# Linear attention with a sign-weight projection: where the next span's LayerNorm affines stand on VectorE

## What is computed

```python
xn = _layernorm(x, axis=-1)
x = x + _L0_attn_ref(xn, Wq, Wk, Wv, Wo, Wb, bb) + _L0_ffn_ref(xn, weights, scale, bias)
...
def _L0_attn_ref(x, Wq, Wk, Wv, Wo, Wb, bb):
    q = (x @ Wq).reshape(B, L, H, Dh)
    k = (x @ Wk).reshape(B, L, H, Dh)
    v = (x @ Wv).reshape(B, L, H, Dh)
    beta = jax.nn.sigmoid(x @ Wb + bb)
    q = _l2norm(q)
    k = _l2norm(k)
    scores = jnp.einsum('blhd,bthd->bhlt', q, k)
    scores = scores * beta.transpose(0, 2, 1)[:, :, None, :]
    mask = jnp.tril(jnp.ones((L, L), dtype=scores.dtype))
    scores = scores * mask
    out = jnp.einsum('bhlt,bthe->blhe', scores, v).reshape(B, L, Dm)
    return out @ Wo
...
def _L0_ffn_ref(x, weights, scale, bias):
    w = (weights >= 0.0).astype(x.dtype) * 2.0 - 1.0
    y = jnp.einsum('bsi,oi->bso', x, w)
    y = y * scale + bias
    y = jnp.clip(y, -MAX_VAL, MAX_VAL)
```

## Time and profile before

| what | us |
|---|---|
| three runs | 1038.15, 1105.11, 1131.73 |
| their median | 1105.11 |
| profiled execution | 1037.92 |
| its span, slowest core (core 4) | 1035.6 |
| its spans, all cores | 1025.6 to 1035.6 |
| PE busy with matmuls | 863.0 (83%) |
| VectorE (DVE) busy | 476.4 (46%) |
| ScalarE (ACT) busy | 280.0 (27%) |

### The profile page before, as it was taken

The page is one execution under the profiler, slowest core; times in us unless marked ns, Lnnn a source line. Parts: engine busy times, 40 slices in busy tenths (PEclk is TensorE's granted clock), DMA queues, the critical chain, the costliest instruction groups (busy, mean ns, idle before and its releaser), DMA issues.

```text
span 1035.6 us, 14710 instructions; the slowest of 8 cores (1025.6 to 1035.6 us)
## 1 busy us (share of the span) xinstructions
PE 863.0 (83%) x5228; PEld 388.9 (38%) x5320; DVE 476.4 (46%) x900; ACT 280.0 (27%) x521; POOL 62.0 (6%) x97
## 2 busy tenths in 40 slices
PE   0008978998999988998999988998989988998995
PEld 0003344433443344433443334433543344434442
DVE  1022375624852365525663365525762365523662
ACT  0003355124122323134132323134223323134110
POOL 9200010000000000000000000000000000000001
PEclk9999977999999999999899989999999989999998
DMA  8962030230134003230134003330134003300135
GB/s 159 168 121 82 0 102 22 59 105 1 41 74 131 1 1 83 62 103 1 41 79 126 1 1 82 61 103 1 41 80 125 1 1 82 82 1 1 41 82 122
DMA packets 21126, 63.90 MB, mean 62 GB/s; under 512 B 3648, under 2 KB 3648, under 8 KB 21056
## 3 DMA queue, kind: packets, MB, share of 16 engines
q0 software_dynamic: 11840, 29.40, 16.9%
q1 hardware_dynamic: 9216, 33.56, 9.1%
HBM read 54.60 MB, written 16.78 MB: 69 GB/s over the span
## 4 chain that ended last, share of the span: by engine, by line
PE 76%; DVE 7%; DMA 4%; ACT 4%; issue 3%; POOL 3%; DVEq 1%; ACTq 1%; POOLq 0%
PE pBig L500 23%; PE pBig L835 12%; PE pBig L625 11%; PE pBig L817 9%; PE T L692 5%; DMA scale_pp<-fsc 4%; PE T L766 4%; PE T L521 4%; DVE sT L784 3%; PE pBig L828 2%; DVE vt L653 2%; PE T L748 2%; PE T L559 1%; ACT xnT L472 1%; PE T L703 1%
## 5 line engine op out<-in xcount | busy, mean ns | idle before, releaser
L784 DVE TENSOR_TENSOR sT<-T,mask 128x512 bf16<-128x512 f32 x256 | 164.4, 684 | 106.0 <-PE T L766 106.0
L835 PE MATMUL pBig<-signT,xnT 128*128 128x512 bf16 x474 | 123.9, 401 | 5.3 <-issue 3.2
L817 PE MATMUL pBig<-Wo,ctxT 128*128 128x512 bf16 x490 | 122.2, 388 | 2.0 <-issue 1.1
L500 PE MATMUL pBig<-xnT,Wq 128*128 128x512 bf16 x503 | 121.6, 385 | 1.7 <-ACT xnT L472 1.4
L500 PE MATMUL pBig<-xnT,Wk 128*128 128x512 bf16 x504 | 119.8, 380 | 0.4
L625 PE MATMUL pBig<-Wv,xnT 128*128 128x512 bf16 x497 | 109.9, 379 | 1.5 <-issue 1.1
L755 ACT COPY fb<-T 128x512 f32<-128x512 f32 x64 | 38.3, 599 | 267.0 <-PE T L748 266.3
L692 PE MATMUL T<-sT,vt 128*64 128x256 bf16 x512 | 65.5, 300 | 29.1 <-DVE sT L784 26.2
L466 PE MATMUL T<-ident,xn_nat 128*128 128x128 bf16 x256 | 18.9, 230 | 81.3 <-DVE xn_nat L454 79.1
L861 POOL DMA_DIRECT2D outt<-x x32 | 27.7, 864 | 843.3 <-DVE outt L852 843.3
L513 DVE TENSOR_TENSOR sT<-qT 128x512 bf16<-128x512 bf16 x64 | 27.2, 426 | 108.4 <-ACT qT L508 56.1
(11 more groups left out here) (83 smaller groups left out, 778.2 us busy)
## 6 DMA issues: line engine op xcount, KB each, us to landing
xf<-x SPq DMA_DIRECT2D x32, 512.0 KB, 7.4
outt<-x POOLq DMA_DIRECT2D x32, 512.0 KB, 5.5
out<-outt SPq DMA_DIRECT2D x32, 512.0 KB, 2.7
outt<-wf POOLq DMA_DIRECT2D x8, 512.0 KB, 4.7
Wq<-wq POOLq DMA_DIRECT2D x8, 256.0 KB, 11.9
Wk<-wk POOLq DMA_DIRECT2D x8, 256.0 KB, 24.2
Wv<-wv POOLq DMA_DIRECT2D x8, 256.0 KB, 32.1
Wo<-wo POOLq DMA_DIRECT2D x8, 256.0 KB, 37.4
```

Of the source, the lines that this page charges most:

```text
L500: (lambda wname, dt_, di, pb, sp: lambda e: e.matmul(ps[pb][:, :], w_slice(wname, di, dt_ * 128, (dt_ + 1) * 128), sb["xnT"][:, (sp * NT + ...
L784: (lambda h01, st_base, gsc=gscs[h01]: lambda e: e.tensor_tensor(sb["sT"][:, (st_base + h01 * 2) * CK:(st_base + h01 * 2 + 2) * CK], ps[gs ...
L817: (lambda cs_, pt, lt, dc, pw: lambda e: e.matmul(ps[pw][:, :], sb["ctxT"][:, (cs_ * (H // 2) + pt) * CK + lt * 128: (cs_ * (H // 2) + pt) ...
L835: (lambda di, dc, span_lt, pyp, sp: lambda e: e.matmul(ps[pyp][:, :], sb["xnT"][:, (sp * NT + di) * SPAN + span_lt * 128: (sp * NT + di) * ...
```

## The change

The affines of the next span are issued all four together, right behind the eight foldings of V (L653) and ahead of the first chunk, instead of one at a time in the head loop. `emit_ln_affine(lt)` becomes `emit_ln_affines(b_, s_)`, which holds the loop over four blocks; the list `pending_affines` goes.

```diff
-        def emit_ln_affine(lt):
-            P.op("vector",
...
+        def emit_ln_affines(b_, s_):
+            for lt in range(4):
+                P.op("vector",
+                     (lambda lt: lambda e: e.tensor_scalar(
+                         sb["xn_nat"][:, lt * D:(lt + 1) * D],
+                         sb["xf32"][:, lt * D:(lt + 1) * D],
+                         sb["rstd"][:, lt:lt + 1], sb["murstd"][:, lt:lt + 1],
+                         ALU.mult, ALU.subtract))(lt),
+                     reads=[f"xf32.{lt}", "rstd", "murstd"], writes=[f"xn_nat.{lt}"], tag="affine")
...
-            for _lt in range(4):
-                emit_ln_affine(_lt)
+            emit_ln_affines(0, 0)
...
                 if i == 6 and pending_lnfin is not None:
                     emit_ln_finish(*pending_lnfin)
-                    pending_affines.extend(range(4))
...
                          reads=[f"vt.{lt}.{dc}", f"fkb.{lt}"],
                          writes=[f"vt.{lt}.{dc}"], tag=f"vfold{lt}.{dc}")
+
+            if pending_lnfin is not None:
+                emit_ln_affines(*pending_lnfin)
 
             for ci in range(2):
...
                     pop_D(1)
-                    if 1 <= p_ <= 4 and pending_affines:
-                        emit_ln_affine(pending_affines.pop(0))
```

More of the change, by code:

```diff
@@ L405, in build_program @@
     store_total = {0: 0, 1: 0, 2: 0, 3: 0}
-    pending_affines = []
     for b in range(NB):
```

## The result

The changed kernel takes 1056.71 us in the median (1056.02 to 1058.36, 8 runs); the kernel before takes 1038.27 us in the median of six. The ratio of the comparison is 1.0178, with a 95% interval of 1.0166 to 1.019. So the change makes the kernel slower by 1.8%, clear of the noise and under the 2% line. Runs in which one die ran at a lower clock, from which the median of 1105.11 us ahead of the prediction came, are left out of every time and ratio in this text; the profiled execution of before (1037.92 us) was the right base.

What follows compares the result with a forecast made beforehand. PE was taken as bound, waiting for VectorE's first mask. Core 3: 1031.7 - 4.7 (old clock cost) + 15.4 (wait less loop gain) + 13.8 (clock) = 1056.2; latest core 1057, plus 2.3 gives 1059 us; range 1048 to 1070.

Steps and rivals of the forecast that it cites:

- The wait: Start of the head loop, spans two to seven: PE's 1.94 us wait for the first mask lengthens by 3.0 us.
- What the loop gives back: Head loop without the four affines, spans two to seven: gains 0.44 us a span.
- The first span: First span, VectorE the bound: masks start 3.0 us later, the next four head pairs are shorter; cost taken as 0.
- The clock: PE's granted clock after the longer wait: drops in each of spans two to seven, 2.3 us each, 13.8 us for six.
- The sum: Whole execution: core 3 at 1056.2 us, core 4 at 1054.5, latest core at 1057, plus 2.3 around the span: 1059 us.
- The clock costs nothing more: Rival: after the longer wait, low clock periods end about as soon as now, only the wait counts; 1053 us, chance 0.16.
- The clock costs more than seen: Rival: the low clock reaches further into the head loop, adding 8 us over six spans; 1067 us, chance 0.18.
- The loop pays the wait back: Rival: VectorE limits the head loop, so removing four affines returns the wait's cost; about 1038 us, chance 0.05.
- The account in which the old falls have another cause: Spans two to seven: present clock drops stay and six new ones come on top; core 4 at 1064.8 us, no chance given.

Runs made afterwards that it cites:

- double dose: The changed kernel with each of the four affines executed twice at its new place: 1078.69 us, ratio 1.0399.
- half dose: The kernel before with two of the four affines ahead of the first mask and two left in the loop: 1042.51 us, ratio 1.003.
- The mirror: Kernel before with affines behind `murstd`, and the second chunk's four folds of V moved from ahead of the first mask into the loop: 1010.04 us, ratio 0.9714.
- its own run: The kernel before with the affines put ahead of the masks in the first span alone: 1041.67 us, ratio 1.0037.
- the filler runs: Wo group's 8 matmuls repeated in PE's wait: twice in the changed kernel, 1041.01 us; once in the kernel before, 1024.3 us; once with affines behind `murstd`, 1024.8 us.

## Why the prediction was right or wrong

The time was forecast at 1059 us and came out at 1056.71, inside the range. The direction was right. The chance was not placed well: 0.52 went to slower by more than 2%, and the ratio is 1.0178. Two per cent of 1038 is 21 us and I forecast 21; measured were 18.4 us between the kernels in repeated runs. Point by point, in the mean of the cores:

*The wait.* Forecast 3.0 us a span, 18.0 in six; measured 3.07 and 18.5. Right, and the double and the half dose follow the same rule: 3.07 and 1.63 us for what was put ahead of the first mask. The mirror agrees, but cannot measure the pitch: it took away four folds of 0.6 us, and only the wait of 1.93 us was there to be won (PE resumes 2.01 us earlier).

*What the loop gives back.* Forecast 0.44 us a span from the last span against the seventh; the loops without a fall give 0.37, 2.2 us in six and not 2.6. Right in kind and nearly in size. The last span differs from the seventh by a little more than its affines: the low clock in both is nearly but not quite the same.

*The first span.* Forecast 0; measured 1.2 us, as its own run confirms. This step was wrong: "I take 0, the value of the row without idle". VectorE was the bound only with the affines in the loop. Without them PE, which runs this stretch at 1.2 GHz, was nearly as slow, and VectorE waits 0.34, 0.47 and 0.53 us in the pairs that were shortened. How much of this is PE and how much the four shared banks `T`, no run separates. A row without idle says which engine is the bound now, and not by how much.

*The clock.* This is the term that was mis-sized. The mechanism was right: after 5 us a fall comes every time, in all six spans of every core, and no longer than before (the double dose has the same loop). Its price was put at "2.3, near the middle", 13.8 us for six; it is 11.7 / 6 = 1.95 us in the mean, since falls as dear as 2.90 us are the rarer ones: single falls cost 1.2 to 2.8 us. With 5.1 us paid before, the difference is 6.7 and not the 8.7 that my 13.8 would leave. The two cores that I forecast show it: core 3 came to 1053.5 us and not 1056.2 (its falls went from 4.6 to 9.0 us, not to 13.8), core 4 to 1050.4 us and not 1054.5 (12.6 us after). Core 4 had also paid 11.5 us before and not 10.3, since its fifth span has a second fall and loses 4.1 us, not 2.90. The latest core, core 0, happens to pay 14.1 us. That the time came within 3 us of the forecast owes something to this.

*A term that was missing.* The second chunk gains 1.7 us, as low stretches of its own of about 1.6 us each come less often (14.1 us at the low clock in six spans before, 10.7 after). I had read the rows up to the second chunk's transposes and taken the rest as unchanged. It is unchanged in instructions, but not in clock. The eighth span's loop gains 0.6 us in the same way. The half dose (5 us there) shows how large this term can be.

*The sum.* Forecast 18.0 - 2.6 + 8.7 = 24.1 us in the mean; measured 18.5 - 2.2 + 6.7 - 1.7 + 1.2 - 0.6 = 21.9, of 21.7 in the spans. On the slowest core before, it is less, since that core had much of the low clock already (forecast 21.4, measured 20.2). And the profiled execution of before was a quick one in its mean (1029.6, where 28 others have 1031.3 on average), while the changed kernel's mean over nine executions is 1051.5. That is the step from 21.7 to about 20 us that no single profile could show.

*The rivals.* "The clock costs nothing more" would have been 1053 us; the filler runs rule it out. "The clock costs more than seen" falls with the loops themselves: single falls cost at most 2.8 us, and with the double dose the six cost no more in the mean (11.6 us for 11.7). "The loop pays the wait back" falls with the loops without a fall (0.37 us a span), and holds for most of the first span, where 2.1 of 2.9 us came back. The account in which the old falls have another cause than the wait of 1.94 us and stay, 1064.8 us for core 4, falls too: that core came to 1050.4 us, and with that wait filled the kernel before has one fall in 48 spans instead of 22.

## What to carry to other kernels

Work moved in an engine's queue costs at its new place what waits behind it, however idle the engine is on average: look for the wait of the bound engine that already ends with this queue, and keep out of the queue ahead of that point whatever that wait does not need. The idle time ahead of another wait of the same queue (here 6.22 us, before `fkb`) takes the same work for next to nothing. And put on the critical queue first only what the next consumer reads: half of the folds was enough, and worth more than everything else tried.

## What the runs showed of the hardware

A wait of 1.93 us on PE is enough to bring the granted clock from 2.4 to 1.2 GHz in 22 of 48 spans, at 1.3 to 2.9 us each (4.1 where it fell twice). Waits of 3.56, 5.01 and 8.07 us bring it down in every span of every core, at no higher price: 1.95 us in the mean with 5.01 us, 1.9 with 8.07. Filling the gap with repeated matmuls keeps it at 1.00 in 47 of 48 spans before and 44 of 48 after, and makes both kernels faster: by 13.5 us with 56 useless matmuls, by 15.7 with 112. The Trainium skill, "TensorE: Matmul & The Clock Gate", section "Why this matters for your kernels", advises against long idle gaps between bursts of matmuls; the trace agrees with the advice, but falls come here already after gaps shorter than it warns of.

Which spans are hit seems to depend on timing as fine as 1 to 2 us: moving four instructions in the first span alone shifted the mean of the cores by some 4 us (1035.3 for 1031.3), three times what the first span itself lost. So a few microseconds of a difference between two versions of this kernel can be such luck, and only the mean over cores and repeated runs tells.
